# First loads divided over two queues, warm-up products, a copy moved ahead, VectorE copies removed, in a three-stage decoder kernel

## The chip, the cores and the metric

One NeuronCore of one Trainium2 chip runs the whole kernel. The metric is the device time of one execution in microseconds (us), lower is better. The engines are TensorE (PE in the rows, its weight loads PEld), VectorE (DVE), ScalarE (ACT), GpSimd (POOL) and SyncE (SP, here only an issuer of transfers).

## The reference

A decoder block on x of 8 x 256 x 256 (8 batches of 256 tokens, width 256), all in float32:

```python
x = x + attn(layernorm(x))        # u; xf = u@WB.T, xb = u@WBf.T (edges keep u)
                                  # gamma = sigmoid(xf@w1 + xb@w2 + b); y = gamma*(xf+xb) + (1-gamma)*u
x = x + xattn(layernorm(x), ctx)  # q, k rotated; scores * decay mask; times v
x = x + ffn(layernorm(x))         # rms norm, router, top 2 of 8 experts,
                                  # h = val*silu(gate), down, weighted sum, + skip
```

## The kernel before

The program is one block with a hand-written instruction stream for each engine, tied by semaphores. There are three stages.

Stage A (`step_a`, 11 steps) does the first line for one batch per step, in a software pipeline: layer-norm statistics on VectorE (L794 to L801), the power on GpSimd (L691 to L697), u on ScalarE (L481), transposes on TensorE (L1124), projection (L1132, L1134, L1138), gate (L499), sum (L823) and the statistics of the next norm (L829 to L837). Beside that, ScalarE squares two halves of one expert's up weights in each step (L466, called from `square`), for the scale of a later split of the weights into two fp16 parts. Stage B (`step_b`, 12 steps) does the cross attention in the same way, with the router's scores (L546, L1202), and splits the first eight halves of up weights (L513 on ScalarE writes the high part, L872 on VectorE the low part); down weights are split by `down_high` (L535) and `down_low` (L880). Then a chain on VectorE (L997 to L1068) sorts the pairs of token and expert into 39 slots of 128 rows. TensorE sums the slot table at L1291, with products that only occupy it between them (`keep_clock`, L1192). Stage E (`step_e`, 42 steps) works one slot per step: up product in three parts (L1315, `up`), silu (L651, L671), product (L1101), split into high and low (L667, L673, L1107 to L1110), transposes (L1342), copies (L1085, L657), down product (L1366 to L1370), scaling (L645) and an indirect DMA that adds the rows to `out` (L770). The rows of a slot are fetched by an indirect DMA (L759, `take`) and transposed by a DMA (L447); those of slot 0 are transposed by TensorE (L1298) and copied by ScalarE (L628).

What orders the work around the change:

- SP's queue starts with x of batch 0, all constants `cst` (L374, 209 KB), x of batches 1 and 2, two tiny loads, x of batch 3, the first up weights (L376), the other x and up weights. ScalarE's queue has four loads (L453): the two projection weights and, broadcast to all partitions, w1 and w2. VectorE waits for all four (L804) before it does the products of weights at L808 to L816 and goes on to the statistics of batch 1.
- `wait_apart` (L305 to L310) waits and then issues a one-element copy on VectorE, ahead of the statistics' next instruction.
- `steps(eng, step, n, lo, hi)` writes steps 0 to lo and hi to n out and runs those between in a hardware loop. ScalarE's stages A and B are written out throughout, VectorE's are looped from step 4 to 8, TensorE's E from 6 to 38.
- At the end of stage B (step 10, batch 7) ScalarE casts the high part of the normed rows (`xn_high`, L541, which waits for the store of the batch before), and then copies the transposed rows out of PSUM (L592) for the router.
- ScalarE does three down high parts (L626), then waits for the transposes of slot 0 (L627), copies them (L628) and does the rest (L629). From the third high part on, each waits for the low part of two before, which VectorE does at L1070, behind two register loads (L1069).
- GpSimd ends with a wait for the last added rows (L775).

## Time and profile before

| | us |
| --- | --- |
| median of 3 runs | 423.23 (423.17 to 423.8) |
| the profiled execution, its own time | 424.23 |
| its span, first to last instruction | 422.3 |
| stage A and its head | 0 to 52 |
| stage B | 52 to 138.5 |
| routing and slot table | 138.5 to 156 |
| stage E, first up product to last add | 162 to 416 |

The profiled execution took 1.93 us beyond its span and 1.00 us more than the median. TensorE is busy for 372.5 us (88% of the span), VectorE 265.5, ScalarE 242.7, GpSimd 181.2. A row of the timeline has the start, the duration, the engine and the line in `kernel.py`, and in brackets how long the engine was idle before it and what ended that. The chain of waits is followed back from the last instruction, at each step to what released it.

### The profile page before, as it was taken

To read this page: it belongs to the slowest core of one execution; us is meant where nothing else is said; L and a number is where in the kernel's file an instruction comes from. 1 tells how busy PE (TensorE), PEld (TensorE's weight loads), DVE (VectorE), ACT (ScalarE), POOL (GpSimd) and SP (SyncE) were. 2 spreads that over 40 slices of the span, in tenths; PEclk is the share of its full clock that TensorE was granted. 3 is DMA by queue.
4 is the path that set the end of the run, shared out by engine and by line. 5 is a ranking of instruction groups with operands and counts; after the bars stand their busy time and mean duration, and the time that the engine had idled before them with its cause. 6 is when DMAs were issued, how large, how long until landed. Compare 5 with 4: busy or idle time off the path is not lost.

```text
span 422.3 us, 9783 instructions
## 1 busy us (share of the span) xinstructions
PE 372.5 (88%) x2465; PEld 263.7 (62%) x2466; DVE 265.5 (63%) x712; ACT 242.7 (57%) x451; POOL 181.2 (43%) x184
## 2 busy tenths in 40 slices
PE   1799999999998076899899999999999999999970
PEld 0578888889886042565566666666666666656650
DVE  1898888898796984878756664444445444544530
ACT  2599966867766375778566544544444444445430
POOL 2534645764756012056345444334434433443321
PEclk9999999999999566999999999999999999999996
DMA  7999873452234602133343343434343333433621
GB/s 230 407 424 406 302 244 106 140 160 75 75 106 170 193 0 64 28 64 54 62 74 54 60 76 53 72 64 75 52 73 63 60 65 67 71 53 63 61 27 12
DMA packets 45159, 47.59 MB, mean 113 GB/s; under 512 B 25680, under 2 KB 40912, under 8 KB 43984
## 3 DMA queue, kind: packets, MB, share of 16 engines
q1 hardware_dynamic: 36768, 36.02, 26.8%
q0 software_dynamic: 7536, 10.52, 16.0%
q10 hardware_dynamic: 832, 0.79, 0.6%
q8 instruction: 9, 0.15, 0.1%
q14 instruction: 14, 0.11, 0.1%
HBM read 32.83 MB, written 9.50 MB: 100 GB/s over the span
## 4 chain that ended last, share of the span: by engine, by line
PE 67%; DVE 10%; issue 7%; ACT 5%; DMA 4%; POOL 3%; DVEq 1%; ACTq 1%; POOLq 0%
PE bank L1315 32%; PE bank L1342 6%; PE bank L1366 5%; PE bank L1367 5%; PE bank L1368 5%; PE bank L1230 2%; PE bank L1171 2%; DMA arena<-in_w 2%; PE bank L1239 2%; DMA xrow_hbm<-front 1%; ACT arena L466 1%; DVE arena L905 1%; PE bank L1192 1%; PE bank L1370 1%; PE bank L1124 1%
## 5 line engine op out<-in xcount | busy, mean ns | idle before, releaser
L1315 PE MATMUL bank<-expert_w,arena 128*128 x702 | 154.8, 367 | 2.7 <-ACT arena L628 2.1
L770 POOL DMA_INDIRECT out<-arena,add_idx x39 | 67.3, 1725 | 133.0 <-ACT arena L645 133.0
L1315 PEld LDWEIGHTS bank<-expert_w,arena 128*128 128x128 f16 x702 | 67.5, 99 | 65.1 <-issue 13.6
L1101 DVE SCALAR_TENSOR_TENSOR arena<-bank,dn_small,arena 128x512 f32<-128x512 f32 x78 | 45.3, 580 | 21.0 <-PE bank L1315 18.7
L759 POOL DMA_INDIRECT arena<-xrow_hbm,take_idx x39 | 39.5, 1012 | 39.1 <-DVE add_idx L1053 22.3
L1085 DVE COPY arena<-bank 128x1024 f16<-128x1024 f16 x39 | 26.9, 689 | 43.6 <-PE bank L1342 43.6
L1366 PE MATMUL bank<-expert_w,arena 128*128 x195 | 53.2, 273 | 1.2 <-DVE arena L1085 0.9
L667 ACT ACTIVATE arena<-arena 128x512 f16<-128x512 f32 x39 | 24.5, 629 | 51.3 <-DVE arena L1101 51.3
L1367 PE MATMUL bank<-expert_w,arena 128*128 x195 | 53.2, 273 | 0.0
L1368 PE MATMUL bank<-expert_w,arena 128*128 x195 | 53.1, 273 | 0.0
L1107 DVE TENSOR_TENSOR arena<-arena 128x512 f16<-128x512 f32 x39 | 27.0, 692 | 27.6 <-ACT arena L667 27.6
L1342 PEld LDWEIGHTS bank<-ident,arena 128*128 128x128 f16 x429 | 26.7, 98 | 14.1 <-ACT arena L673 6.4
L651 ACT ACTIVATE arena<-bank,small 128x512 f32<-128x512 f32 x39 | 26.8, 687 | 11.2 <-PE bank L1315 10.0
L1342 PE MATMUL bank<-ident,arena 128*128 128x128 f16 x429 | 30.3, 219 | 3.3 <-ACT arena L673 1.4
L728 POOL TENSOR_TENSOR arena<-arena 128x512 f32<-128x512 f32 x16 | 23.2, 1457 | 19.4 <-DVE arena L948 14.7
L673 ACT ACTIVATE arena<-arena 128x192 f16<-128x192 f32 x39 | 14.1, 363 | 30.3 <-DVE arena L1101 30.3
L645 ACT ACTIVATE arena<-bank,arena 128x256 f32<-128x256 f32 x39 | 18.5, 474 | 22.6 <-issue 18.1
L872 DVE SCALAR_TENSOR_TENSOR expert_w<-expert_w,small 128x1408 f16<-128x1408 f32 (+1 forms) x14 | 26.4, 1888 | 1.2 <-ACT expert_w L513 1.2
L1124 PE MATMUL bank<-cst,arena 128*128 128x128 f32 x96 | 15.7, 289 | 10.7 <-ACT arena L481 10.1
L1366 PEld LDWEIGHTS bank<-expert_w,arena 128*128 128x128 f16 x195 | 19.1, 98 | 7.5 <-issue 3.3
L466 ACT ACTIVATE arena<-expert_w,front 128x1408 bf16<-128x1408 f32 x16 | 23.5, 1468 | 0.0
L1367 PEld LDWEIGHTS bank<-expert_w,arena 128*128 128x128 f16 x195 | 19.0, 98 | 4.6
(190 smaller groups left out, 667.1 us busy)
## 6 DMA issues: line engine op xcount, KB each, us to landing
expert_w<-in_wup SPq DMA_DIRECT2D x8, 1408.0 KB, 17.6
expert_w<-in_wdn SPq DMA_DIRECT2D x8, 640.0 KB, 4.7
rows<-in_x SPq DMA_DIRECT2D x8, 256.0 KB, 8.6
arena<-in_ctxT SPq DMA_DIRECT2D x8, 256.0 KB, 3.2
xrow_hbm<-front SPq DMA_DIRECT2D x8, 256.0 KB, 2.2
out<-rows SPq DMA_DIRECT2D x8, 256.0 KB, 2.7
rows<-in_wup SPq DMA_DIRECT2D x1, 1408.0 KB, 6.2
expert_w<-in_wdn SPq DMA_DIRECT2D x16, 64.0 KB, 4.8
```

Source lines behind the costliest of these rows:

```text
L466: nc.scalar.activation(squares, raw_chunk(e * 2 + c), ACT.Square, scale=ns_s[:, c:c + 1], accum_out=sq[:, ds(e * 2 + c, 1)]).then_inc(s_sq, 1)
L651: nc.scalar.activation(sg[:, 0:HA], bank[0][:, 0:HA], ACT.Silu, scale=descale[:, ds(e, 1)]).then_inc(s_sg, 1)
L759: pool.indirect_dma_start(out=xs_row[:, i % 2], out_offset=None, in_=xrow_hbm, in_offset=bass.IndirectOffsetOnAxis(ap=take_idx[:, i:i + 1] ...
L770: pool.indirect_dma_start(out=out, in_=yt[:, i % 2], in_offset=None, out_offset=bass.IndirectOffsetOnAxis(ap=add_idx[:, i:i + 1], axis=0), ...
L1085: V.tensor_copy(hT[:, 0:8], hT_bank[0]).then_inc(s_hTa, 1)
L1101: V.scalar_tensor_tensor(out=hh[:, cols], in0=src, scalar=h_scale[:, ds(e_h, 1)], in1=sg[:, cols], op0=ALU.mult, op1=ALU.mult).then_inc(s_ ...
L1107: V.tensor_tensor(hs_low, hh[:, cols], hs_high[:, cols], ALU.subtract).then_inc(s_hlo, 1)
L1315: last = T.matmul(bank[q][:, 0:n], xsT[:, slot, 2 * a + c], up_w[:, ds(w0 + c * UPC + w * 2 * H + lo, n)], start=m == 0, stop=m == len(pro ...
L1342: last = T.transpose(hT_bank[c // 8][:, c % 8], hs[:, c * P:(c + 1) * P], ident16[:, :])
L1366: T.matmul(y, hT[:, c], dn_at(w_dn, c, 0), start=c == 0, stop=False)
L1367: T.matmul(y, hT[:, c], dn_at(w_dn, c, 1), start=False, stop=False)
L1368: T.matmul(y, hT[:, NH if c == NH - 2 else NH + 1 + c], dn_at(w_dn, c, 0), start=False, stop=False)
```

## The change

The constants are reordered so that `ones` and `last` come last, and loaded in two parts; w1 and w2 are loaded by SP between the two, ahead of x of batch 1; ScalarE's queue keeps the two projection weights. TensorE does ten products of 128 columns on the constants at its start and two more in step 1. All of `wait_apart`'s copies become plain waits, and VectorE's stages A and B are written out. In step 10 of stage B ScalarE copies the transposed rows before it casts the high part. Two down high parts instead of three stand ahead of the copy of slot 0's rows. VectorE loads one expert number instead of two ahead of its low parts, scales slot 0's pairs between them, and those of slot 1 at the end of step 1; in odd steps it reuses a loaded number. `keep_clock` in the slot table has 192 columns instead of 256, and three products instead of two behind it. TensorE's loop in stage E starts at step 4. The wait for the last added rows moves from GpSimd to SP.

```diff
-    for names in ((("ident", P), ("ones", P), ("last", P), ("edge", 2), ("mhalf", NT), ("minus", NT)),
+    for names in ((("ident", P), ("edge", 2), ("mhalf", NT), ("minus", NT), ("ones", P), ("last", P)),
...
-        def wait_apart(eng, *waits):
-            for s, v in waits:
-                eng.wait_ge(s, v)
-            nc.vector.tensor_copy(spare[:, 0:1], spare[:, 0:1])
...
-        E_STEPS = (NSLOT + 3, 6, 38)
+        E_STEPS = (NSLOT + 3, 4, 38)
...
             load_x(0)
-            sp.dma_start(cst[:, :], consts).then_inc(s_cst, 16)
+            first = at_const["ones"][0]
+            sp.dma_start(cst[:, 0:first], consts[:, 0:first]).then_inc(s_cst, 16)
+            for dst, src in ((w1_s, w1.partition_broadcast(P)), (w2_s, w2.partition_broadcast(P))):
+                sp.dma_start(dst, src).then_inc(s_fw, 16)
+            sp.dma_start(cst[:, first:n_const], consts[:, first:n_const]).then_inc(s_ones, 16)
...
                 sp.dma_start_transpose(xsT[:, i % 2], xs[:, i % 2, 0:4 * P]).then_inc(s_xsT[i % 2], 16)
+            sp.wait_ge(s_add, 16 * NSLOT)
...
-            for dst, src in ((wb_s[:, :, 0:D], wproj), (w1_s, w1.partition_broadcast(P)),
-                             (wbf_s[:, :, 0:D], wproj2), (w2_s, w2.partition_broadcast(P))):
+            for dst, src in ((wb_s[:, :, 0:D], wproj), (wbf_s[:, :, 0:D], wproj2)):
...
-                    act.wait_ge(s_xn, b + 1)
-                    xn_high(b)
+                    if r < NBATCH + 2:
+                        act.wait_ge(s_xn, b + 1)
+                        xn_high(b)
                     act.wait_ge(s_tr3, b + 1)
...
                                          ACT.Copy).then_inc(s_xnT, 1)
+                    if r == NBATCH + 2:
+                        xn_high(b)
...
-            down_high(DN_DRAIN, DN_DRAIN + 3)
+            down_high(DN_DRAIN, DN_DRAIN + 2)
             act.wait_ge(s_first, 1)
             nc.scalar.activation(xsT[:, 0], hT_bank[0][:, 0:4], ACT.Copy).then_inc(s_xsT[0], 16)
-            down_high(DN_DRAIN + 3, DN_GATHER)
+            down_high(DN_DRAIN + 2, DN_GATHER)
...
+            pool.wait_ge(s_ones, 16)
             steps(pool, step_b, *B_STEPS)
...
-            pool.wait_ge(s_add, 16 * NSLOT)
...
-                    wait_apart(dve, (s_st, b + 1))
+                    dve.wait_ge(s_st, b + 1)
...
-            steps(dve, step_a, *A_STEPS)
+            steps(dve, step_a, A_STEPS[0], A_STEPS[0], A_STEPS[0])
...
-            first_experts = [dve.snap(dve.value_load(tile_e[0:1, n:n + 1], min_val=0, max_val=NE - 1)) for n in range(2)]
-            down_low(DN_DRAIN, DN_GATHER)
+            load_expert("pair", 0)
+            down_low(DN_DRAIN, DN_DRAIN + 2)
             dve.wait_ge(s_ysc, 4)
+            scale_pairs(0, 0)
+            down_low(DN_DRAIN + 2, DN_GATHER)
...
                 if live(r, 1, NSLOT):
-                    e_h = first_experts[0] if r == 1 else dve.snap(dve.value_load(tile_e[0:1, ds(i, 1)], min_val=0, max_val=NE - 1))
+                    if k == 0 and r > 0:
+                        load_expert("h", at(it, k, 1)[0])
+                    else:
+                        expert["h"] = expert["pair"]
+                    e_h = expert["h"]
...
+                    if r == 1:
+                        load_expert("pair", 1)
+                        scale_pairs(it, k)
...
             pe.wait_ge(s_cst, 16)
+            def keep_clock(n, cols=512, moving=None):
+                moving = cst_b if moving is None else moving
+                for _ in range(n):
+                    T.matmul(bank[3][:, 0:cols], ident, moving[:, 0:cols], start=True, stop=True)
+            keep_clock(10, P, cst)
...
                     transposes(bank[slot], lambda j, c: ut[:, 2 * slot + j, c * P:(c + 1) * P]).then_inc(s_tr, 1)
+                    if r == 1:
+                        keep_clock(2, P, cst)
...
-                    keep_clock(1, 256)
+                    keep_clock(1, 192)
             last.then_inc(s_tab, 1)
-            keep_clock(2)
+            keep_clock(3)
             pe.wait_ge(s_xs[0], 16)
```

## Rows read from the trace of the kernel before

**Rows 1.** Busy time by stage; columns: start:end, us, busy time (instructions), clock, DMA share, GB/s

```profile
17.10:52.00 34.90, 34.34 (x164) 28.35 (x164) 29.77 (x135) 34.84 (x66) 18.30 (x29) 1.00 0.98 391
56.00:125.00 69.00, 68.08 (x371) 60.25 (x370) 57.97 (x134) 48.53 (x77) 41.56 (x47) 1.00 0.37 119
162.10:206.00 43.90, 41.73 (x273) 24.13 (x274) 32.92 (x58) 31.75 (x50) 16.91 (x11) 0.93 0.29 53
206.00:402.00 196.00, 194.68 (x1463) 127.40 (x1461) 101.04 (x229) 95.41 (x196) 83.10 (x63) 1.00 0.39 64
```

**Rows 2.** Timeline of the head and of stage A on ScalarE; start us, us, engine line

```profile
10.53 0.43 DVE L808 CUSTOM_DVE_ANT_0 bank<-front,arena 128x256 f32<-128x256 f32 x1 [4.09 <-DMA arena<-in_w]
...
13.13 0.74 DVE L794 BATCH_NORM_STATS2 small<-rows 128x6 f32<-128x256 f32 x2
...
16.03 1.09 ACT L481 ACTIVATE arena<-rows,small 128x256 f32<-128x256 f32 x2 [5.17 <-POOL small L697]
...
17.03 1.45 ACT L466 ACTIVATE arena<-expert_w,front 128x1408 bf16<-128x1408 f32 x1
...
21.78 1.46 ACT L466 ACTIVATE arena<-expert_w,front 128x1408 bf16<-128x1408 f32 x1
```

**Rows 3.** DMA of the head: load of w1 and w2, landing of `in_wup`, bytes moved so far

```profile
arena<-in_w ACTq DMA_DIRECT2D x2, 128.0 KB, 7.0
...
DMA to landing us min/median/max: 8.9/17.6/27.9
...
0.00:7.50 7.50, 0.00 (x0) 0.01 (x1) 1.30 (x10) 1.70 (x4) 2.17 (x10) 1.00 0.54 174
...
0.00:10.50 10.50, 1.09 (x4) 0.73 (x5) 1.30 (x10) 3.03 (x7) 2.46 (x11) 1.00 0.70 228
```

**Rows 4.** VectorE in stage A: first statistics of two batches, and the copies

```profile
29.75 0.75 DVE L794 BATCH_NORM_STATS2 small<-rows 128x6 f32 x2
...
35.26 0.75 DVE L794 BATCH_NORM_STATS2 small<-rows 128x6 f32 x2 [0.46 <-issue]
...
L310 DVE COPY spare<-spare x40: 153/154/155, 5.9 to 131.5; 128x1 f32<-128x1 f32 x40
```

**Rows 5.** Timeline at the end of stage B, ScalarE

```profile
135.22 0.63 ACT L541 ACTIVATE front<-arena 128x512 f16<-128x512 f32 x1 [0.69 <-DMA xrow_hbm<-front]
...
135.75 0.58 ACT L592 ACTIVATE arena<-bank 128x512 f32<-128x512 f32 x1
```

**Rows 6.** Chain of waits, slot table and first slots; start us, us, what

```profile
151.39 1.03 PE bank L1192 x2
...
162.18 5.31 PE bank L1315 x12
...
171.95 2.27 PE bank L1315 x12
```

**Rows 7.** Timeline around the first slot's rows; in brackets the idle time before

```profile
159.46 4.39 DVE L880 SCALAR_TENSOR_TENSOR expert_w<-expert_w,dn_small 128x768 f16<-128x768 f32 x4 [1.41 <-issue]
...
159.70 0.40 PE L1298 MATMUL bank<-ident,arena 128*128 128x128 f16 x4 [2.25 <-DMA arena<-xrow_hbm,take_idx]
...
160.51 0.94 ACT L535 ACTIVATE expert_w<-expert_w,dn_small 128x768 f16<-128x768 f32 x1 [4.13 <-DVE expert_w L880]
...
161.36 0.58 ACT L628 ACTIVATE arena<-bank 128x512 f16<-128x512 f16 x1
...
167.71 0.75 DVE L1101 SCALAR_TENSOR_TENSOR arena<-bank,dn_small,arena 128x512 f32<-128x512 f32 x1 [3.72 <-PE bank L1315]
```

**Rows 8.** Busy time by stretch around the first products of the experts

```profile
154.60:161.30 6.70, 3.25 (x27) 1.62 (x25) 3.89 (x12) 2.57 (x4) 2.06 (x2) 1.00 0.13 40
161.40:168.20 6.80, 6.02 (x15) 2.27 (x16) 2.88 (x6) 4.22 (x6) 1.89 (x2) 0.50 0.24 58
```

**Rows 9.** The last instructions of GpSimd: timeline row, and the block's end (L64)

```profile
411.81 1.55 POOL L770 DMA_INDIRECT out<-arena,add_idx  x1 [2.92 <-ACT arena L645]
...
L64 POOLq DRAIN  x1: 6520/6520/6520, 415.6 to 415.6; - x1
```

39 lines of the change are left out of this document (21 added, 18 removed).

## The prediction

> **What bounds the kernel now.** I read the busy time by stage first, then the chain of waits, then the timeline where the chain leaves TensorE, and last what the final instructions wait for. In stage A ScalarE has work for 34.84 of 34.90 us and TensorE for 34.34: ScalarE's stream of u, squares and copies sets the pace, and what can be won there is its start. In stage B TensorE has work for 68.08 of 69.0 us, in stage E from 206 us on for 194.68 of 196 [rows 1]. In these three stretches nothing that VectorE saves can shorten the kernel by more than the 0.06, 0.9 and 1.3 us left over. The slack lies in four other places: the head, where ScalarE's first squares start only at 17.03 [rows 2]; the slot table; the head of stage E, where TensorE's mean clock is 0.93 [rows 1]; and the end, where GpSimd's last instruction takes 6.52 us after everything has landed [rows 9].
>
> **1. The head.** VectorE idles 4.09 us until 10.53, for the load of w2, the last of ScalarE's queue. From there everything follows in line: products of weights, statistics of batch 1 at 13.13, u of batch 1 at 16.03, squares at 17.03 [rows 2]. The two loads of w1 and w2 took 7.0 us in the median from issue to landing [rows 3]. By the code, ahead of w2 and with it there are now x of batch 0 (256 KB), the first constants (162 columns, 81 KB), w1 and w2 (128 KB each), the two projection weights (256 KB each), and GpSimd's zeros for `out` (128 KB): 1.26 MB, when both queues advance alike. Before, 228 GB/s over 10.5 us make 2.39 MB moved when w2 was there; 174 GB/s over 7.5 us make 1.30 MB [rows 3]. So w2 lands at about 7.5, and 7.8 with what the SP queue moves beside it: 2.7 us earlier. x of batch 1, now behind 384 KB more, has until 7.8 + 2.6 = 10.4 (the 2.6 from 10.53 to 13.13) and costs nothing while it lands before that. U of batch 1 comes at 13.3. Then the squares wait for the up weights: the first landed 8.9 us after its issue [rows 3], at about 14.7 by the chain of SP's issues, and the bytes ahead of it are the same; that leaves 2.3 us. The second pair of squares stood at 21.78 [rows 2]; its weights come 1.44 MB and four loads of x (1.05 MB, partly moved by then) later, at 391 GB/s [rows 1] between 19 and 21. I take 19.8: 2.0 us gained. Ends: 0.4 (w2 only issued earlier) and 2.9.
>
> The ten warm-up products run while TensorE has nothing to do (1.09 us of work in the first 10.5 us [rows 3]); even at 0.3 us each they are over by 8 and cost nothing. They may let the first projections run at the full clock, but the next step waits for u of batch 1.
>
> **2. VectorE in stage A.** The stream moves 2.0 us earlier only if VectorE keeps up. Its loop takes 5.51 us from batch 5 to batch 6 [rows 4], ScalarE's step 21.78 - 17.03 = 4.75 [rows 2]. VectorE ran ahead before and was caught up with slowly; started earlier with this pace it would become the limit near the end. Written out it loses the 0.46 us of idle time at the loop's turn [rows 4], and each plain wait saves about half of a 0.154 us copy, since the copies overlap. Four per step make 0.3 us; so the step falls to some 4.7 and stays under ScalarE's. Gain by itself 0, but it is the cover of part 1.
>
> **3. Stage B.** 0.92 us of TensorE's idle time is the most that fewer copies can give [rows 1]; I take 0.3. At its end the reordered copy makes the cast of the high part (L541, at 135.22) wait for L592, 0.58 us long, whose own start at 135.75 is held by L541's 0.63 [rows 5]. They change places: the router's operand comes about 0.5 earlier, the low part on VectorE, two down low parts and the first link of the routing chain behind it about 0.3 to 0.5 later, since VectorE, not the score, is last there. I take 0.3 lost: together 0, ends 0.9 gained and 0.6 lost.
>
> **4. Slot table.** Each occupying product of 256 columns stands 1.03 us in the chain [rows 6], five of them, at half the clock. 192 columns make 0.77: up to 5 x 0.26 = 1.3, but the columns that VectorE and ScalarE prepare meanwhile come hardly faster. I take 0.5, ends 0 and 1.1. The third product behind the table falls into idle time before 159.70 and costs nothing.
>
> **5. The copy of slot 0's rows.** The transposes end at 160.10 (159.70 + 0.40). ScalarE copies at 161.36, because its third high part starts only at 160.51, after the first low part at 159.46, which stood behind two register loads of 1.41 us together [rows 7]. With two high parts ahead, ScalarE is free and copies at 160.15: 1.2 us, ends 1.0 and 1.4. The third and fourth high parts follow under the up product.
>
> **6. The clock at the first products.** From 161.40 to 168.20 the clock is 0.50, that is 1.2 GHz, after a stretch in which TensorE worked 3.25 of 6.7 us, most of it early, and 1.00 (2.4 GHz) was granted [rows 8]. The first 12 products take 5.31 us, the same 12 in the next slot 2.27 [rows 6]. Now there are three products of 512 columns before the gap, 1.2 us of it are gone by part 5, and I expect the clock to stay: 3.04 us less for the products. Not all of it arrives: L1101 at 167.71 had idled 3.72 us for them [rows 7], but VectorE's low parts last until 163.85 (159.46 + 4.39) and ScalarE must do a high part of up weights and one of 0.94 us between silu and the next cast. I take half of it, 1.6; ends 3.0 and -0.3.
> By the Trainium skill (TensorE: Matmul & The Clock Gate, Part 1) the activity monitor is free-running and does not restart with a kernel, so where it falls varies from run to run. One trace cannot show that; by this rule some executions would keep the 1.6 us and others not, at a mean gain of half.
>
> **7. Slot 1's scale.** One more register load and its product now stand in step 1 on VectorE, ahead of a low part, in a stretch where VectorE is busy. Two loads took 1.41 us [rows 7], so one 0.7: I take 0.6 lost, ends 0.8 and 0. The reused numbers of later steps change nothing, for TensorE sets that pace [rows 1]; nor does its longer loop.
>
> **8. The end.** GpSimd issues the last transfer from 411.81 to 413.36, waits for it to land, and only then starts its DRAIN of 6.52 us at 415.6, which releases the block's end at 422.1 [rows 9]. With the wait on SP the DRAIN can start at 413.4: 2.2 us, if its length is its own. If it must wait for the transfer too, 0. The other engines had drained by then. No row shows a DRAIN with a transfer out, so both ends stay; I take 2.2, as nothing was in flight for those 6.52 us, and they can hardly be a wait for data.
>
> **Sum.** 2.0 + 0 + 0.5 + 1.2 + 1.6 - 0.6 + 2.2 = 6.9 us. The profiled execution would come to 424.23 - 6.9 = 417.3; it stood 1.00 above the median of the runs, so from there 423.23 - 6.9 = 416.3.
>
> **Rivals.**
> - The clock falls all the same. TensorE still has nothing to do for about 2.3 us between the third product and the first up product, but for the 0.40 of the transposes; for it speaks that 161.40 came after such a gap, against it that this one is shorter by 2 us. Without the 1.6: 417.9. Chance 0.17.
> - The head gives next to nothing. x, weights and constants share the same 16 DMA engines, and if the landing of w2 depends on all that has been issued and not on its place, only its issue comes earlier, 0.4 instead of 2.0: 417.9. Against it, 2.39 MB had moved before w2 landed, and half of them now stand behind it. Chance 0.10. The Trainium skill (DMA: Bandwidth & Descriptors, Issuing engines are not separate DMA queues) speaks for it: it says that issuing on several engines saves only the sequencer's time. By this rule the gain is that of the issue alone; no row of before tells the two apart.
> - The DRAIN waits for the transfer, and ends when it did: 416.3 + 2.2 = 418.5. Chance 0.13.
> - Slower: the expert numbers. VectorE now takes them in another order in every slot of stage E; if that puts one load, 0.7 us [rows 7], ahead of the copy of the transposed rows (L1085), TensorE's down product waits. It decides as soon as more than TensorE's present idle time (1.3 us in 32 slots [rows 1]) is passed; with 0.3 us of the 0.7 in each of 38 slots it is 11.4 us: 416.3 + 11.4 = 427.7. Against it, the odd steps have a load fewer. Chance 0.03.
> - The parts cancel or are not there at all (the 0.6 us lost at stage B, nothing at the head, table and end, no clock): 1.2 - 0.6 - 0.6 = 0, 423.2. Chance 0.02.
>
> **The numbers.** The forecast, all main parts within their ends and a time of 413.5 to 419, has 0.55. Its fast end has the whole 3.0 of the clock, 2.9 at the head and 0.9 in stage B, 11 us in all, which is unlikely together; I stop at 413.5. Two of the three weaker rivals at once give about 420. So the range is 413.5 to 420.3. A change of 0.2% (0.85 us) is what measuring this kernel can tell from none. These cases give faster by more 0.95, within it 0.02, slower by more 0.03.
>
> **What would show it.** L808 starts near 7.8 and L466 first near 14.8; stage A's last square ends near 50 instead of 52; L541 of batch 7 comes after L592; L628 starts within 0.1 us of the end of L1298; the clock reads 1.00 through the first products, and 12 of them take 2.3 us; the DRAIN starts at the end of the last L770 and lasts 6.5. Wrong would be: L808 after 9.5, L794 of batch 1 idle on its x, VectorE idle time in ScalarE's stream, a stretch of 0.50 after slot 0's copy, a DRAIN of 8.7 us, or slots from 206 us on that take more than 6.1 us each.

## The result, and the profile after

The changed kernel takes 421.26 us in the median (420.57 to 421.45, five runs), the kernel before 423.23 (422.68 to 423.8, five runs): ratio 0.9948, 95% interval 0.9936 to 0.9959, so 2.0 us faster. The forecast was 416.3 with a range of 413.5 to 420.3: the sign was right, the size was not. The profiled execution took 421.26 us with a span of 419.4. Before it was 424.23 with 422.3, so the two spans differ by 2.9 us, of which 1.0 is that the profiled execution of before stood above its median. The balance below is that of the spans.

Busy time by stage of the changed kernel, columns as in [rows 1]:

```profile
17.00:52.00 35.00, 34.52 (x161) 28.19 (x159) 28.21 (x111) 33.50 (x66) 17.35 (x28) 0.96 0.99 392
160.00:206.00 46.00, 41.25 (x296) 25.36 (x294) 36.53 (x61) 34.34 (x53) 19.55 (x12) 1.00 0.30 55
206.00:402.00 196.00, 193.88 (x1450) 126.08 (x1449) 99.42 (x228) 95.05 (x196) 81.95 (x62) 1.00 0.37 63
9.30:16.20 6.90, 3.48 (x21) 2.74 (x20) 6.63 (x30) 2.24 (x4) 2.92 (x5) 1.00 1.06 387
16.30:19.60 3.30, 3.30 (x10) 2.56 (x9) 1.97 (x8) 2.73 (x5) 2.79 (x6) 0.50 1.03 418
161.40:168.20 6.80, 4.95 (x25) 2.15 (x24) 4.28 (x7) 5.44 (x9) 0.94 (x1) 1.00 0.26 58
```

Two things stand out. The clock is 1.00 where it was 0.50 in the first products of the experts (161.4 to 168.2, [rows 8]). And at the head there is now a stretch at 0.50, from 16.3 to 19.6, behind one at 1.00. The timeline of the head, columns as in [rows 2], the warm-up products first:

```profile
4.64 4.64 PE L1151 MATMUL bank<-cst 128*128 128x128 f32 x20 [4.64 <-DMA cst<-in_consts]
...
9.11 0.43 DVE L809 CUSTOM_DVE_ANT_0 bank<-front,arena 128x256 f32<-128x256 f32 x1 [3.24 <-DMA arena<-in_w]
...
14.55 1.09 ACT L479 ACTIVATE arena<-rows,small 128x256 f32<-128x256 f32 x2 [4.07 <-POOL small L698]
...
15.55 1.45 ACT L464 ACTIVATE arena<-expert_w,front 128x1408 bf16<-128x1408 f32 x1
...
20.31 0.41 ACT L497 ACTIVATE small<-bank,small 128x1 f32<-128x1 f32 x2 [1.28 <-PE bank L1164]
...
21.60 1.46 ACT L464 ACTIVATE arena<-expert_w,front 128x1408 bf16<-128x1408 f32 x1
```

VectorE starts the products of weights at 9.11 instead of 10.53, and ScalarE its first squares at 15.55 instead of 17.03. But the second pair of squares starts at 21.60, against 21.78 [rows 2]: within one step, 1.3 of the 1.5 us are gone. The rows put the idle 1.28 us ahead of L497 down to TensorE.

The end of stage B, first slot and end of the program, to be held against [rows 5, 7, 9]:

```profile
135.12 0.60 ACT L591 ACTIVATE arena<-bank 128x512 f32<-128x512 f32 x1 [0.89 <-PE bank L1142]
...
135.61 0.62 ACT L539 ACTIVATE front<-arena 128x512 f16<-128x512 f32 x1
...
136.27 0.69 DVE L958 TENSOR_TENSOR front<-arena,front 128x512 f16<-128x512 f32 x1 [1.51 <-ACT front L539]
```

```profile
158.84 2.15 DVE L881 SCALAR_TENSOR_TENSOR expert_w<-expert_w,dn_small 128x768 f16<-128x768 f32 x2 [0.78 <-issue]
...
159.79 0.40 PE L1322 MATMUL bank<-ident,arena 128*128 128x128 f16 x4 [1.14 <-DMA arena<-xrow_hbm,take_idx]
...
160.29 0.60 ACT L629 ACTIVATE arena<-bank 128x512 f16<-128x512 f16 x1 [3.51 <-PE bank L1322]
...
164.13 0.75 DVE L1116 SCALAR_TENSOR_TENSOR arena<-bank,dn_small,arena 128x512 f32<-128x512 f32 x1 [0.20 <-PE bank L1339]
```

```profile
411.13 1.55 POOL L772 DMA_INDIRECT out<-arena,add_idx  x1 [2.93 <-ACT arena L646]
...
L64 POOLq DRAIN  x1: 8303/8303/8303, 410.9 to 410.9; - x1
```

ScalarE's copy (L629) starts 0.10 us after the transposes end (159.79 + 0.40), and L1116 at 164.13, not 167.71. GpSimd's DRAIN is recorded from 410.9 with 8.30 us, near the 8.7 that the forecast had named as a sign of being wrong. But the issue of the last transfer on the same engine lies within it and ends at 412.68 (411.13 + 1.55): from there to the DRAIN's end at 419.2 it is 6.5 us, as before, now beside the last additions instead of behind them.

The starts of a few instructions divide both spans (all from timelines; negative is a gain):

| part | before | after | change | forecast |
|---|---|---|---|---|
| up to the last keys of stage B (L1171, now L1200) | 117.71 | 117.34 | -0.37 | -2.0 |
| last keys to the routing chain (L997, now L999) | 20.83 | 21.59 | +0.76 | 0 |
| to the transposes of slot 0's rows (L1298, now L1322) | 21.16 | 20.86 | -0.30 | -0.5 |
| to slot 0's second transposes (L1342, now L1366) | 11.48 | 8.40 | -3.08 | -2.8 |
| slot 0's to slot 1's transposes | 6.38 | 6.97 | +0.59 | +0.6 |
| slot 1's to slot 8's | 45.99 | 46.53 | +0.54 | 0 |
| slot 8's to slot 36's, the steady stretch | 171.98 | 173.15 | +1.17 | 0 |
| to the issue of the last transfer (L770, now L772) | 16.28 | 16.30 | +0.02 | 0 |
| to the end of the span | 10.49 | 8.27 | -2.22 | -2.2 |

Four terms of the sum (copy and clock together, slot 1's scale, the end) came as forecast. What is missing is 1.6 us at the head, 0.8 at the end of stage B, and 1.7 in stage E, where nothing was expected.

### The profile page after: what moved, and what is told of

Same layout as the page of the kernel before. It is cut to its first block, busy times and chain, and to the rows that moved or that the text cites. A ratio compares the mean times of both kernels' runs of the same rounds, so it can differ in the third digit from the quotient of the medians.

```text
span 419.4 us, 9669 instructions
## 1 busy us (share of the span) xinstructions
PE 375.3 (89%) x2491; PEld 268.6 (64%) x2492; DVE 265.6 (63%) x672; ACT 242.4 (58%) x451; POOL 180.3 (43%) x184
## 4 chain that ended last, share of the span: by engine, by line
PE 71%; ACT 8%; DVE 8%; issue 5%; DMA 4%; POOL 1%; POOLq 0%; SPq 0%; DVEq 0%; ACTq 0%
PE bank L1339 32%; PE bank L1366 5%; PE bank L1390 5%; PE bank L1391 5%; PE bank L1392 5%; ACT arena L464 3%; PE bank L1200 3%; PE bank L1254 3%; PE bank L1263 2%; ACT arena L479 2%; DMA arena<-in_w 2%; PE bank L1142 1%; PE bank L1151 1%; PE bank L1160 1%; PE bank L1158 1%
## 5 line engine op out<-in xcount | busy, mean ns | idle before, releaser
L772 POOL DMA_INDIRECT out<-arena,add_idx x39 | 67.5, 1732 | 128.1 <-ACT arena L646 128.1
L1116 DVE SCALAR_TENSOR_TENSOR arena<-bank,dn_small,arena 128x512 f32<-128x512 f32 x78 | 45.3, 580 | 18.5 <-PE bank L1339 15.9
L1366 PEld LDWEIGHTS bank<-ident,arena 128*128 128x128 f16 x429 | 26.8, 98 | 14.1 <-ACT arena L674 5.8
L1366 PE MATMUL bank<-ident,arena 128*128 128x128 f16 x429 | 30.3, 219 | 3.7 <-DVE arena L1125 1.6
L646 ACT ACTIVATE arena<-bank,arena 128x256 f32<-128x256 f32 x39 | 18.5, 473 | 22.4 <-issue 18.3
L729 POOL TENSOR_TENSOR arena<-arena 128x512 f32<-128x512 f32 x16 | 21.8, 1365 | 21.6 <-DVE arena L950 16.9
L873 DVE SCALAR_TENSOR_TENSOR expert_w<-expert_w,small 128x1408 f16<-128x1408 f32 x14 | 27.4, 1958 | 1.2 <-ACT expert_w L511 1.2
L1124 DVE TENSOR_TENSOR arena<-arena 128x128 f16<-128x128 f32 x39 | 11.4, 293 | 16.7 <-ACT arena L674 16.7
```

The costliest lines, as they stand in the source:

```text
L772: pool.indirect_dma_start(out=out, in_=yt[:, i % 2], in_offset=None, out_offset=bass.IndirectOffsetOnAxis(ap=add_idx[:, i:i + 1], axis=0), ...
L873: V.scalar_tensor_tensor(out=part(n, 1), in0=split_source(n), scalar=up_scale[:, ds(n, 1)], in1=part(n, 0), op0=ALU.mult, op1=ALU.subtract ...
L1116: V.scalar_tensor_tensor(out=hh[:, cols], in0=src, scalar=h_scale[:, ds(e_h, 1)], in1=sg[:, cols], op0=ALU.mult, op1=ALU.mult).then_inc(s_ ...
L1366: last = T.transpose(hT_bank[c // 8][:, c % 8], hs[:, c * P:(c + 1) * P], ident16[:, :])
```

## The experiments

First theory: the head's gain is lost because the clock, raised early by the warm-up products, falls again in TensorE's idle time ahead of the second batch; stage E loses by where TensorE's loop now starts; the end of stage B by the reordered cast. The rivals are in the expectations. Each kernel below is the changed kernel with the edit shown, unless it says otherwise. What is read from each is in this table (us; from starts in the timelines). "Keys" is from L809's start to the first keys of stage B, "B end" from the last keys to L999, "slot 0" from L1322 to the first L1366, "steady" from slot 8's L1366 to slot 36's; before has the same places under its own line numbers. In the second column, how many instructions later than in the changed kernel TensorE's loop of stage E comes to lie, as counted from the edit ahead of it.

| run | TensorE code | L809 | keys | B end | slot 0 | steady | median (runs) | ratio to before |
|---|---|---|---|---|---|---|---|---|
| before | own | 10.53 | 41.80 | 20.83 | 11.48 | 171.98 | 423.23 | |
| after | 0 | 9.11 | 42.97 | 21.59 | 8.40 | 173.15 | 421.26 (5) | 0.9948 |
| e1_loop6 | 0, loop from 6 | 8.89 | 42.90 | 21.26 | 9.46 | 174.44 | 422.67 (12) | 0.9977 |
| e2_nowarm | -48 | 9.29 | 42.84 | 21.22 | 8.40 | 172.04 | 419.63 (4) | 0.9909 |
| e3_gap | +28 | 8.89 | 42.96 | 21.27 | 8.40 | 172.03 | 421.26 (5) | 0.9947 |
| e4_order | 0 | 8.65 | 42.90 | 20.19 | 8.40 | 173.13 | 419.62 (6) | 0.9920 |
| e5_pad28 | +28 | 8.88 | 42.99 | 21.30 | 8.39 | 172.33 | 420.84 (6) | 0.9957 |
| e6_up1 | +28 | 8.61 | 41.59 | 21.28 | 8.39 | 172.30 | 418.89 (6) | 0.9898 |
| e7_three_ahead | 0 | 9.32 | 43.39 | 21.32 | 8.89 | 172.91 | 422.13 (4) | 0.9967 |
| e8_end_only | own | 10.25 | 41.70 | 20.29 | 10.50 | 172.03 | 420.93 (6) | 0.9944 |
| e9_two_behind | -4 | 8.41 | 42.97 | 21.38 | 9.67 | 172.67 | 420.55 (4) | 0.9927 |
| e10_three_mended | +28 | 8.63 | 41.59 | 20.50 | 9.49 | 172.28 | 420.71 (7) | 0.9946 |
| e11_scale_too | +28 | 9.07 | 41.79 | 20.66 | 8.39 | 172.53 | 418.79 (6) | 0.9902 |
| e12_fill | +40 | 9.15 | 41.81 | 21.56 | 8.39 | 172.41 | 418.31 (6) | 0.9879 |
| e13_loop6_pad28 | +28, loop from 6 | 9.29 | 42.98 | 22.95 | 9.49 | 172.02 | 420.42 (4) | 0.9917 |
| e14_pad8 | +8 | 9.06 | 42.94 | 22.02 | 9.49 | 171.70 | 420.97 (4) | 0.9932 |
| e15_copies_back | 0 | 8.73 | 43.04 | 20.83 | 8.39 | 174.27 | 422.17 (12) | 0.9969 |
| e16_up1_alone | 0 | 8.64 | 41.60 | 21.39 | 8.39 | 173.26 | 420.09 (6) | 0.9929 |
| e17_no_warmup_mended | -36 | 9.24 | 41.92 | 20.24 | 8.39 | 172.03 | 417.12 (5) | 0.9845 |

The medians carry less than the stretches do: of one kernel the times spread by 0.4 to 5 us (last section), so each verdict is taken from the stretch that the edit touches. The stretches have a limit of their own: there is one profiled execution of each kernel.

### e1_loop6: TensorE's loop starts at step 6 again

```diff
-        E_STEPS = (NSLOT + 3, 4, 38)
+        E_STEPS = (NSLOT + 3, 6, 38)
```

> The changed kernel (421.26 us) with one line back as it was: TensorE's loop of stage E starts at step 6 again (E_STEPS = (NSLOT + 3, 6, 38)), not at step 4. From slot 8 to slot 36 the kernel before takes 395.53 - 223.55 = 171.98 us between transposes, the changed one 394.83 - 221.68 = 173.15. Theory (the place where the loop starts costs it): the stretch is back at 172.0 and the time at 420.1 (419.8 to 420.5). Rival 1 (VectorE's changed loads of the expert numbers, or what it does at other times, delays something in each turn): the stretch stays at 173.1 and the time at 421.3. Rival 2 (the loss drifts with the program and its clock from run to run): the stretch is neither, and the gaps of 0.38 to 0.40 us ahead of the up product stand at other turns.

The steady stretch took 174.44 us: not back, but 1.3 worse. 1.4 us more were lost behind slot 36 (17.68 us to the last transfer's issue instead of 16.30): the clock was at 0.50 from 410.5 to 413.8, in the last down product. The start of the loop is not what costs; the waits of TensorE from 206 to 402 us say what kind of loss it is (engine, line, waited for: us, times, longest), first of this kernel:

```profile
PE bank L1339 <- issue: 2.4, 9, 0.5
```

"Issue" is time in which no semaphore is waited for. Nine pauses of TensorE's own, up to 0.5 us, ahead of the second part of an up product, 2.4 us in all. The changed kernel has such pauses too, too short for this view: in its timeline the last down product of a slot and the first product of that part, which start 0.11 us apart when nothing holds them, lie 0.38 to 0.40 us apart at slots 9, 13, 17 and so on to 33, and up to 0.21 at the others. In e1_loop6 it is every second slot (a turn of the loop is two), 0.41 to 0.72.

### e2_nowarm: no warm-up products at the head

```diff
-            keep_clock(10, P, cst)
-                    if r == 1:
-                        keep_clock(2, P, cst)
```

> The changed kernel without its 12 warm-up products at the head. Theory (the head's gain of 1.4 us was lost because the clock, raised early by these products, falls in TensorE's idle stretch of 2.34 us ahead of the second batch's transposes, so that two projections run at half clock): without them the first projection is slower by 1 to 2 us at half clock, but the second one meets the full clock; the time is 420.9 to 421.6, the second pair of squares starts at 21.0 to 21.6. Rival 1 (the warm-up products are worth their price): half clock until 18 us, second pair of squares at 21.7 to 22.2, time 421.5 to 422. Rival 2 (the head's gain was lost in the arrival of the weights, not in the clock): no change of the time, 421.3, and the gate's first activation waits for a DMA or for ScalarE's squares, not for TensorE.

419.63, better than expected, but not for the reason given. Steady is 172.04, which is 1.1 of the 1.6 us; the keys come 42.84 behind L809, as good as in the changed kernel. The second pair of squares started at 21.64. The row behind it, on ScalarE's timeline, names another wait than TensorE:

```profile
19.24 0.41 ACT L497 ACTIVATE small<-bank,small 128x1 f32<-128x1 f32 x2
...
21.64 1.47 ACT L464 ACTIVATE arena<-expert_w,front 128x1408 bf16<-128x1408 f32 x1 [1.02 <-DMA expert_w<-in_wup]
```

### e3_gap: products in TensorE's idle time at the head

```diff
                     project(slot, 0)
+                    if r == 2:
+                        keep_clock(7, P, cst)
```

> The changed kernel with 7 more products of 128 columns (about 0.3 us each, from x6 in 1.49 us for three of them at either level and x4 in 0.61 us for two at full clock) behind the first projection, into the bank that the next projection overwrites: they fill 2.1 of TensorE's idle 2.34 us ahead of the second batch's transposes. Theory (the clock falls because of that idle stretch): the granted clock stays full through 16.25 to 19.67 us, the two projections take 2.0 us instead of 3.8, the gate's activation starts at 19.0 instead of 20.31, the second pair of squares at 20.3 instead of 21.60, and the time is 420.0 (419.8 to 420.6). Rival 1 (the clock's rise and fall there does not hang on TensorE's work): half clock at the same place, 421.3. Rival 2 (the gain at the head is taken back by another wait later in stage A): second pair of squares at 20.3, but the last squares and the keys of stage B as in the changed kernel, 421.3.

The first half of the expectation came true. The clock stays at 1.00, L497 starts at 18.73. And it is worth nothing: ScalarE's timeline again, and the clock:

```profile
18.73 0.39 ACT L497 ACTIVATE small<-bank,small 128x1 f32<-128x1 f32 x2
...
21.35 1.47 ACT L464 ACTIVATE arena<-expert_w,front 128x1408 bf16<-128x1408 f32 x1 [1.25 <-DMA expert_w<-in_wup]
```

```profile
9.30:16.20 6.90, 4.85 (x33) 4.26 (x32) 6.63 (x30) 2.45 (x4) 3.12 (x5) 1.00 1.03 377
16.30:19.60 3.30, 3.30 (x17) 2.88 (x16) 2.22 (x9) 3.30 (x9) 2.60 (x6) 1.00 1.06 430
```

The squares waited 1.25 us for the up weights of the second expert. With the clock held, the wait that had stood right beneath TensorE's comes out, and the keys are 42.96 behind L809. The first theory for the head falls. The second: these weights lie behind all the rows of x in SP's queue; from 10 us on the DMA engines are full (shares of 1.03 to 1.06 in the rows of this kernel and of the changed one), and moving w1 and w2 between queues changes nothing of the bytes ahead of them. The landings say the same. In the kernel before these weights were issued at 8.67 and landed at 21.0 (12.3 us later), in e3_gap at 9.48 and 21.3, in the changed kernel at 9.90 and 21.4: 1.2 us of difference in the issue became 0.4 in the landing, and each time 6.7 to 6.8 MB had been moved (319 GB/s over 21.0 us, 318 over 21.3, 317 over 21.4).

### e6_up1 and e16_up1_alone: the second expert's weights earlier

```diff
             load_up(0)
-            for b in range(4, NBATCH):
+            load_x(4)
+            load_up(1)
+            for b in range(5, NBATCH):
                 load_x(b)
-            for e in range(1, NE):
+            for e in range(2, NE):
```

in e6_up1 on top of e3_gap's edit, in e16_up1_alone by itself.

> The kernel e3_gap (full clock through the head) with the second expert's up weights loaded ahead of the rows of batches 5 to 7 instead of behind them. In e3_gap ScalarE's second pair of squares waited 1.25 us for these weights (start 21.35) although the gate's activation came at 18.73; in the changed kernel the same pair starts at 21.60. Theory (the head's 1.4 us are lost at the arrival of these weights, and the clock only hides it): the pair starts at 20.1, the first keys 41.8 us behind L809's start as before (42.97 in the changed kernel, 42.96 in e3_gap), the time 1.1 to 1.2 below e3_gap's. Rival 1 (the next loads come no earlier, since the 16 DMA engines are busy throughout 10 to 40 us): a wait for the third or a later expert's weights, or for the rows of batch 5 to 7, and the first keys still 42.9 behind L809. Rival 2 (TensorE, busy for 9.8 of each 10 us, sets the pace of stage A, so that the gap before the second pair costs nothing): pair at 20.1, keys as in e3_gap.

> The changed kernel with the second expert's up weights ahead of the rows of batches 5 to 7, without the products that fill TensorE's idle stretch. Theory A (the clock's fall there costs once the weights are no longer the limit): gate's activation at 20.3 where the clock falls, first keys 42.8 to 43.0 us behind L809, no gain, 421.3. Theory B (stage A takes it up later, TensorE and ScalarE have slack enough): first keys 41.6 to 42.0 behind L809, time 419.9 to 420.2. In a run where the clock does not fall at the head (it does not in every run of one kernel), both give 41.6.

Both give the whole gain: second pair of squares at 19.72 and 19.75, keys 41.59 and 41.60 behind L809, 1.4 less than in the changed kernel. The weights land at 18.5 and 18.8, with 5.7 and 5.8 MB moved. ScalarE in e6_up1:

```profile
18.45 0.39 ACT L499 ACTIVATE small<-bank,small 128x1 f32<-128x1 f32 x2
...
19.72 1.46 ACT L466 ACTIVATE arena<-expert_w,front 128x1408 bf16<-128x1408 f32 x1
```

So the head's loss is settled: it is the landing of the second expert's `in_wup`. What the fallen clock would cost by itself is not, for in e16_up1_alone's profile it did not fall at the head. e17_no_warmup_mended bounds it below.

### e4_order: the old order at the last batch of stage B

```diff
-                    if r < NBATCH + 2:
-                        act.wait_ge(s_xn, b + 1)
-                        xn_high(b)
+                    act.wait_ge(s_xn, b + 1)
+                    xn_high(b)
                     act.wait_ge(s_tr3, b + 1)
...
-                    if r == NBATCH + 2:
-                        xn_high(b)
```

> The changed kernel with ScalarE's old order at step NBATCH+2 of stage B: the cast of xn ahead of the copy of its transposes. In the profiles the chain from the last cast to the router's bias grew by 0.39 us against the keys of the last batch that came 0.2 to 0.3 earlier, so 0.6 to 0.7 was lost there. Theory (the new order costs it): activation of xnT 0.6 earlier, time 420.7 (420.5 to 421.0). Rival (the loss is the copies that VectorE lost or the arrival of the rows' store, not the order): 421.3, and the cast and the copy change places without the end of the stage moving. The order may be worth something after all, in the opposite direction: 421.5.

The time is 419.62, lower than expected, and B end 20.19 instead of 21.59 (21.27 in e3_gap, profiled in the same series). The casts of batches 6 and 7 (here L539) and the copy (here L590), and VectorE's low part behind the last cast:

```profile
129.38 0.63 ACT L539 ACTIVATE front<-arena 128x512 f16<-128x512 f32 x1 [3.12 <-DMA xrow_hbm<-front]
...
133.68 0.63 ACT L539 ACTIVATE front<-arena 128x512 f16<-128x512 f32 x1 [0.41 <-DMA xrow_hbm<-front]
...
134.21 0.58 ACT L590 ACTIVATE arena<-bank 128x512 f32<-128x512 f32 x1
...
134.34 0.69 DVE L955 TENSOR_TENSOR front<-arena,front 128x512 f16<-128x512 f32 x1 [0.54 <-ACT front L539]
```

The copy can't start before TensorE's transposes end: 0.09 us behind them here (134.12), 0.04 behind them in the changed kernel (135.08). So the cast in front of it sat in idle time and cost the copy nothing; put behind it, it comes 1.1 us later (16.87 behind the last keys here, 17.96 in e3_gap), and VectorE's low part and the chain of routing with it. Over all profiles with the new order B end is 21.2 to 21.6 (21.30 in the median, leaving out e13 and e14, where the clock fell to half earlier in that stretch than in the others); with the old one 20.2 to 20.8, and once 21.56, in e12_fill.

What makes B end vary beside the order is in the timelines too. In all 19 profiles the chain starts 3.3 us behind the cast of batch 7, so the cast is what it hangs on. And ahead of the casts ScalarE waits for the landing of the store before (`xrow_hbm<-front`): of batch 6's cast 3.1 to 3.6 us, but 4.5 and 4.6 in e13_loop6_pad28 and e12_fill. From the cast of batch 6 to that of batch 7 it is 5.26 us in the nine profiles with the new order (5.68 and 5.73 in e13 and e14) and 4.16 to 4.57 in the eight with the old one, e12_fill's 4.16 among them. So the order costs 0.7 to 1.1 us in every one; where in this range depends on when the store of batch 6 lands, since the old order waits for it and the new one is behind it already.

### e5_pad28, e14_pad8, e13_loop6_pad28: only the place of TensorE's code

```diff
+            for _ in range(7):
+                T.matmul(bank[3][0:2, 0:2], ident[:, 0:2], cst[:, 0:2], start=True, stop=True)
             keep_clock(10, P, cst)
```

2 such products in e14_pad8; in e13_loop6_pad28 7, and `E_STEPS` as in e1_loop6.

> The changed kernel with 7 tiny products (2 columns by 2, 28 instructions of TensorE with their weight loads) ahead of the warm-up products: they do nothing but move all later code of TensorE by 28 instructions, as far as the products of e3_gap moved it. From slot 8 to slot 36 the runs so far took 171.98 us (before), 173.15 (after), 173.13 (e4_order, same code of TensorE), 174.44 (loop at step 6), 172.04 (without the warm-up) and 172.03 (e3_gap). Theory (the place of the loop's code alone costs the 1.1 us): the stretch takes 172.0 and the time falls by 1.1 against the changed kernel. Rival 1 (what is gained in e2_nowarm and e3_gap comes from the head or the clock): the stretch stays at 173.1. Rival 2 (the loss is VectorE's, by its expert numbers): 173.1 too, and it would show in e2_nowarm and e3_gap, where it doesn't.

> The changed kernel with 2 tiny products at the head, a displacement of TensorE's later code by 8 instructions. Theory (place of the code): the stretch from slot 8 to slot 36 is one of the values seen so far, between 172.0 and 174.5, and gaps of 0.4 us stand at another set of turns than in the changed kernel (173.15) unless 8 instructions are too few to matter. Rival (e5_pad28's 172.33 was won by the tiny products' other effects at the head): 172.3 here too, since these are the same products.

> e1_loop6 (TensorE's loop of stage E from step 6) with the 7 tiny products of e5_pad28 at the head. Theory (only the place of the code counts): the stretch from slot 8 to slot 36, 174.44 us in e1_loop6, changes by over 0.5 us, most likely down to 172.0 to 172.5, time 1 to 2.4 less than e1_loop6's 422.67. Rival (the start at step 6 is what costs): the stretch stays at 174.4, time 422.7.

Steady took 172.33, 171.70 and 172.02. The last is the clearest: the same edit that made 174.44 of it makes 172.02 once everything lies 28 instructions further on, 2.4 us for seven products of four numbers at the other end of the program. TensorE's waits of 206 to 402 us in e13_loop6_pad28:

```profile
PE bank L1341 <- issue: 0.6, 1, 0.6
```

One pause where e1_loop6 had nine. And all five kernels whose TensorE code lies where the changed kernel's does (after, e4, e7, e15, e16) take 172.9 to 174.3 and have the distance of 0.38 to 0.41 us at every fourth slot; of the ten that start the loop at step 4 elsewhere none has it (the longest distance there is 0.33 us, once), and they take 171.7 to 172.7. Moving the loop's start from 6 to 4 is innocent in this stretch; where its code came to lie costs 1.1 us. Why one place is worse than another no run shows.

### e7_three_ahead and e9_two_behind: the copy, and the clock of slot 0

```diff
-            down_high(DN_DRAIN, DN_DRAIN + 2)
+            down_high(DN_DRAIN, DN_DRAIN + 3)
...
-            down_high(DN_DRAIN + 2, DN_GATHER)
+            down_high(DN_DRAIN + 3, DN_GATHER)
```

```diff
             last.then_inc(s_tab, 1)
-            keep_clock(3)
+            keep_clock(2)
```

> The changed kernel with three high parts ahead of the copy of slot 0's transposes again, as before, instead of two (the third behind it removed). Forecast at record: 1.2 us. Theory: from the start of ScalarE's first part (L1322's product order aside) the copy comes 1.1 to 1.2 later, slot 0's transposes 9.5 to 9.6 behind TensorE's L1322 instead of 8.40, the time 1.2 more than the changed kernel. Rival (the clock is what the copy bought): TensorE idles longer ahead of the first up products, the clock falls as in the kernel before, slot 0's transposes 11.4 behind L1322, the time 3.0 more. Rival 2 (a full clock in some runs and half in others, by how the clock falls against the program): times of the runs spread by 1.5 to 2 us.

> The changed kernel with two products of 512 columns behind the slot table instead of three. In the profiles of the kernel before and of e8_end_only, which have two, TensorE idled 2.24 us ahead of L1298 and the clock stood at half from 161.4 to 168.2 and from 162.4 to 165.8; with three (all runs of the changed kernel but e1_loop6, where it fell from 161.2 to 164.6) it idled 0.8 to 1.14 us and the clock stayed. Theory (the third product keeps the clock through slot 0): the clock falls in slot 0, its transposes come 9.4 to 10.4 us behind L1322 instead of 8.40, the time 1.1 to 1.9 above the changed kernel. Rival (the earlier copy is what keeps it, or it is chance, since e7_three_ahead kept it and e1_loop6 lost it): transposes 8.4 behind, same time as the changed kernel.

With three parts ahead the copy comes 0.51 us later against the transposes than in the changed kernel, not 1.2, slot 0 takes 8.89, and the clock stays. ScalarE in e7_three_ahead, and VectorE's first low part:

```profile
159.19 2.15 DVE L881 SCALAR_TENSOR_TENSOR expert_w<-expert_w,dn_small 128x768 f16<-128x768 f32 x2 [0.77 <-issue]
...
160.08 0.40 PE L1322 MATMUL bank<-ident,arena 128*128 128x128 f16 x4 [0.79 <-DMA arena<-xrow_hbm,take_idx]
...
160.24 0.93 ACT L533 ACTIVATE expert_w<-expert_w,dn_small 128x768 f16<-128x768 f32 x1 [3.11 <-DVE expert_w L881]
...
161.09 0.58 ACT L629 ACTIVATE arena<-bank 128x512 f16<-128x512 f16 x1
```

The third part waits for VectorE, and VectorE now idles 0.77 us ahead of its low parts instead of 1.41 [rows 7], for it loads one number instead of two. The forecast's 1.2 us were right as a sum; 0.65 of them belong to the load that was taken away, only 0.5 to the order of the parts.

With two products behind the table the clock was at half from 160.0 to 163.3, at the first up products of slot 0; these are stretches of e9_two_behind:

```profile
153.10:159.90 6.80, 3.56 (x27) 1.64 (x25) 4.93 (x16) 3.56 (x7) 2.06 (x2) 1.00 0.13 40
160.00:163.30 3.30, 3.30 (x8) 1.18 (x9) 2.04 (x2) 1.81 (x3) 1.71 (x1) 0.50 0.30 60
163.40:168.00 4.60, 3.39 (x17) 1.39 (x15) 2.10 (x5) 3.46 (x6) 0.00 (x0) 1.00 0.18 43
```

Slot 0 took 9.67, the expected size, but the time was not above the changed kernel's (420.55): the code lies elsewhere (-4, steady 172.67, 0.5 less), and in this profile L809 started 0.7 earlier. And three products don't exclude it. The clock fell there in the profiles of all three kernels with two products (before, e8, e9) and in four of fourteen with three (e1, e10, e13, e14), each time for 1.1 us (9.46 to 9.49 against 8.39), 1.3 in e9. The two with three more products ahead of the first up product (e12, e17) kept it; two are too few to prove it.

### e8_end_only: the kernel before with the last wait on SP

```diff
 in GpSimd's program:
-            pool.wait_ge(s_add, 16 * NSLOT)
 at the end of SP's:
+            sp.wait_ge(s_add, 16 * NSLOT)
```

> The kernel before with one part of the change alone: the wait for the last slots' additions into the output stands on SyncE instead of GpSimd. Theory (GpSimd's last drain of 6.5 us runs beside the last scatters, from the issue of the last one on, instead of behind their landing): 2.2 us less than before, 421.0 to 421.4. Rival (the drain waits for the scatters itself, or SyncE's end comes as late): no change, 423.5.

420.93 against 423.25, ratio 0.9944 (0.9931 to 0.9957): 2.3 us, all that the change as a whole brings. The last instructions of GpSimd:

```profile
410.96 1.55 POOL L771 DMA_INDIRECT out<-arena,add_idx  x1 [3.04 <-ACT arena L646]
...
L64 POOLq DRAIN  x1: 8305/8305/8305, 410.7 to 410.7; - x1
```

Span 419.3, so 8.3 us behind the last issue's start, as in the changed kernel, against 10.5 before.

### e15_copies_back: VectorE's copies and loops

e4_order with all five `wait_apart` and both `steps(dve, ...)` loops of stages A and B as before.

> e4_order with VectorE's copies of one column behind its waits and VectorE's loops of stages A and B put back as before. Forecast on record: 0. Theory: first keys to last keys 65.38 us as before instead of 65.26, last keys to L999 20.2 to 20.3 as in e4_order, time within 0.3 of e4_order's 419.6. Rival (the copies and loops sit on the chain at the end of stage B): last keys to L999 20.5 to 20.8, time 0.3 to 0.8 more.

The forecast of 0 is not borne out: 422.17 over twelve runs, ratio 0.9969 (0.9954 to 0.9984) against e4_order's 0.9920. First keys to last keys took 65.38 instead of 65.26 us, B end 20.83 instead of 20.19, slot 0 to slot 1 7.36 instead of 6.97, and steady 174.27 instead of 173.13. The first 0.12 are the copies'. B end is the landings of the stores: the casts of batches 6 and 7 waited 3.50 and 0.67 us for them, against 3.12 and 0.41 in e4_order (e8_end_only has the same copies and a B end of 20.29). The other two lie in stage E, whose VectorE code is the same but for its place. TensorE's code has not moved at all, so its place can't be what costs these 1.5 us. That it is the place of VectorE's code is only a guess: no run moved that alone.

### e10 to e12 and e17: mended versions

e10_three_mended has the edits of e3_gap, e6_up1 and e4_order; e11_scale_too also takes slot 1's number and scale at the start of step 1; e12_fill adds three products ahead of slot 0's first up product; e17_no_warmup_mended is e12_fill without the 19 products at the head.

```diff
-                if live(r, 0, NSLOT) and r > 1:
+                if live(r, 0, NSLOT) and r > 0:
                     load_expert("pair", at(it, k, 0)[0])
...
-                if live(r, 0, NSLOT) and r > 1:
+                if live(r, 0, NSLOT) and r > 0:
                     scale_pairs(it, k)
...
-                    if r == 1:
-                        load_expert("pair", 1)
-                        scale_pairs(it, k)
```

```diff
             last.then_inc(s_first, 1)
+            keep_clock(3, P)
             pe.wait_ge(s_te, 1)
```

> The changed kernel with the three mended places together: products in TensorE's idle stretch at the head (e3_gap), the second expert's weights ahead of the rows of batches 5 to 7 (e6_up1), and ScalarE's old order at the last batch (e4_order). If they add up, the span is that of e6_up1 less the 1.06 us of e4_order: stage B ends (L999) 20.2 behind the last keys instead of 21.3, time 417.8 to 418.0, and the whole forecast of the change (6.9 us against 423.2, so 416.3) is reached but for 1.5 us. Rival (e4_order's gain was its own run's, by the landing of a store): L999 21.3 behind the last keys, time 418.9.

> e10_three_mended with slot 1's expert number and pair scale taken by VectorE at the start of step 1, as before, instead of at its end. Forecast on record for that loss: 0.6 us, and slot 0's period was 6.97 in the changed kernel against 6.38 before. Theory: period 6.38, time 0.6 below e10_three_mended. Rival (the same load now delays VectorE's products of slot 0, since it stands ahead of them and waits for slot 1's rows): slot 0's period 6.4 but its start later by as much, time as e10_three_mended's.

> e11_scale_too with three products of 128 columns between slot 0's transposes (L1322) and its first up product, where TensorE idles 0.94 us. If the clock at the first products is what spreads the times of one kernel by 2 to 4 us from run to run (e5_pad28: 420.0 to 421.0 at a mean granted clock of 0.969 to 0.973, 423.4 and 424.5 at 0.961 and 0.962), these products make the runs agree within 1 us and the median falls by 0 to 1 us. Rival (the spread comes from elsewhere, or the clock falls in another place): the same spread, and the same or a slightly later first up product.

> e12_fill (418.31 us, all places mended) without any of the 19 products at the head. Theory (the clock at the head is worth something once the second expert's weights come early): in e2_nowarm the gate's activation started at 19.24, 9.95 us behind L809, against 9.83 in e12_fill, and the first keys 42.84 behind it; the pair of squares can start 1.0 behind the gate's activation, so the first keys come 41.9 to 42.3 behind L809 instead of 41.81 and the time is 0.1 to 0.5 above e12_fill's. Rival (the products at the head do harm by where they leave the clock later): the same or a lower median and runs within 1 us of each other, 417.5 to 418.3.

The stretches add up: keys 41.59 and B end 20.50 in e10; slot 0 to slot 1 in 6.38 us instead of 6.97 from e11 on, with slot 0 no slower, so the 0.6 us of slot 1's scale were a loss without a return. The medians of e10 and e11 don't show it cleanly (420.71 from 417.39 to 422.01, and 418.79 from 417.3 to 422.34); e12_fill's runs should have agreed within 1 us if the clock at slot 0 was what spreads them. They took 416.84 to 420.4, though in its profile the clock stayed through slot 0: the rival, that the spread comes from elsewhere too, holds. e17 came out below both forecasts: 417.12 (416.01 to 417.41), ratio 0.9845 (0.9832 to 0.9858), 4.1 us below the changed kernel and 6.1 below before, so the warm-up products have no measurable use. That they do harm by the clock, as the rival says, no run shows. Without them the keys come 41.92 behind L809, against 41.59 to 41.81 in the five kernels that have them and the early weights: 0.1 to 0.3 us is all that the clock costs at the head. Between the two profiles e17's is 1.0 us shorter: 1.3 at B end and 0.4 at the steady stretch, less 0.3 at the table and 0.4 in other places. The 1.3 is a landing, not an edit: e12_fill's ScalarE waited 4.63 us for the store ahead of batch 6's cast, e17's 3.15.

```profile
130.30 0.63 ACT L541 ACTIVATE front<-arena 128x512 f16<-128x512 f32 x1 [4.63 <-DMA xrow_hbm<-front]
...
134.46 0.63 ACT L541 ACTIVATE front<-arena 128x512 f16<-128x512 f32 x1 [0.28 <-DMA xrow_hbm<-front]
```

Whether that is also why the medians lie 1.2 us apart is open, for the other executions have no trace.

## Why the prediction was wrong, step by step

- **The head (2.0 forecast, 0.25 at the first keys, 0.37 at the last).** Two sizes failed. L808 was to start at 7.8 and started at 9.11: by 9.1 us 205 GB/s had moved 1.87 MB, not the 1.30 that were to be ahead of w2, so the two queues didn't advance by the share I gave them. In all kernels with the new loads L809 started between 8.41 and 9.32. And the step that lost it all is "its weights come ... between 19 and 21. I take 19.8": they landed at 21.3 to 21.6, where the squares of e1_loop6, e2_nowarm and e3_gap waited for them, as late as the kernel before needed them. What was wrong in it is "partly moved by then": when the first expert's weights landed (7.13 + 8.0 = 15.1), none of these loads had (from there to 21.4, 419 GB/s over 6.3 us are 2.64 MB). The whole 1.44 + 1.05 = 2.49 MB at 391 GB/s are 6.4 us, which gives 21.5; measured 21.4. The trace of before had it: there the first weights landed at 5.79 + 8.9 = 14.7 and the second at 8.67 + 12.3 = 21.0, with the same loads between them. These rows spoke for 21 and not for 19.8. The rival "the head gives next to nothing" (0.10) is what happened, but by another mechanism than its own: w2 did land 1.4 us earlier. By the rule of the Trainium skill (DMA: Bandwidth & Descriptors, Issuing engines are not separate DMA queues), as the forecast read it, only the time of issue would have been gained. Measured, w2 was issued at 2.22 instead of 2.72 and landed at 9.09 instead of 10.50: its place ahead of other loads counted as well.
- **The warm-up products.** "Even at 0.3 us each they are over by 8" was wrong: the ten took 4.64 us, until 9.28, and TensorE's first transposes (L1142) came at 9.07, though u of batch 0 was there at 8.44. "Cost nothing" held all the same, because the first projection waits for VectorE's products of weights: it started 2.26 us behind L809, and 2.27 in e2_nowarm. The next step waited for u of batch 1, as forecast, and the clock's fall at 16.3 in that wait cost nothing beside the landing (e3_gap).
- **VectorE in stages A and B (0).** Stage A kept its pace. Between first and last keys 0.12 us were won (65.26 for 65.38). e15_copies_back says that more hangs on these edits in stage E, by what no step of the forecast looked at.
- **The reordered cast (0.3 lost).** 0.7 to 1.1 were lost. The step's error: "the router's operand comes about 0.5 earlier". The copy's own start was held not by L541's 0.63 but by TensorE's transposes, which end just as the cast does; nothing came earlier, and the cast was later by the wait and the copy. That VectorE and not the score is last there was right: the chain follows the cast by 3.3 us.
- **Slot table (0.5).** 0.3 came. The products took 0.82 each in the chain, not the 0.77 of the forecast (1.03 before). That is 5 x 0.21 = 1.05 us less, of which most did not arrive; which wait took it the runs do not separate.
- **The copy and the clock (1.2 + 1.6).** 3.08 came, as a sum nearly right; the division is above. In part this is luck of the execution that was profiled: before had the clock at half for 6.8 us at slot 0 (161.4 to 168.2), e8_end_only, the same program there, for 3.4 us (162.4 to 165.8), and its slot 0 took 10.50 us. Held against that one the gain is 2.1. The 1.00 us by which the profiled execution of before stood above its median has the same size, but its other executions have no trace. The rival with 0.17, that the clock falls all the same, is true of four of the fourteen profiles with three products. In the Trainium skill (TensorE: Matmul & The Clock Gate, Part 1) the monitor is free-running, so that the clock's changes come at other places from run to run. That clock and time go together some runs show: of e5_pad28 they took 420.0 to 421.0 at a mean clock of 0.969 to 0.973, and 423.4 and 424.5 at 0.962 and 0.961. But e11_scale_too took 417.3 and 419.88, both at 0.973, so the clock is not all of the spread.
- **Slot 1's scale (0.6 lost).** 0.59.
- **The end (2.2).** 2.22, and 2.3 by itself.
- **Stage E ("nor does its longer loop").** This step failed: 1.17 us in the steady stretch, and 0.54 from slot 1 to slot 8. The sign named for it, slots of more than 6.1 us, could not have told: 171.98 / 28 are 6.14 before, 173.15 / 28 are 6.18 now. The first is where TensorE's code lies, shown by three displacements. Of the second I only know that it is also there in e17 and e11 (46.5), and 46.2 in e13_loop6_pad28 and 46.7 in e1_loop6, both with the loop from step 6 instead of from 4 (46.0 before). One piece is a pause of 0.52 us, again "issue", ahead of an up product at 192.93 in e3_gap. The rest stays open.

Together the missing 1.6, 0.8 and 1.7 us and 0.2 at the table, less the 0.3 that slot 0 gave more, are the 4.0 us between 6.9 and the spans' 2.9; the last 1.0 to the medians' 2.0 is the profiled execution of before.

## What to carry to other kernels

Before a load is moved forward, write down the landing of the next one that the same engine needs: with the DMA engines full it depended on the bytes ahead of it, and a gain ends there, however early the first one comes. Here the trace of before had that landing, at 21.0 us. A wait that ends together with another hides it: in the changed kernel the rows blamed TensorE, and taking that away (e3_gap) won nothing and showed the real one. And any edit moves the code behind it: when a loop of many turns changes by a per cent without a wait to account for it, displace the code by a few idle instructions before looking for a cause in the edit.
